# A two-layer kernel with routed adapters: item places a block sooner, column numbers in portions, B remainders last in VectorE's step, last-layer weights rounded in pieces

## Chip, cores and metric

One NeuronCore of a Trainium2 chip. The metric is the device time of one execution in microseconds; lower is better.

## What is computed

64 items of 32 tokens with 512 features pass through two residual layers, all in f32. Cut to what matters:

```python
# layer 0: per item one of 8 matrices, then a linear layer with per-group LoRA
c  = einsum('bsi,boi->bso', x, weight[itok_B_3_7])
x  = x + c @ kernel + bias + lora0(c) + lora_shared(c)
# layer 1: per item one of 16 adapters on gate, up and down of a SiLU layer (512 -> 1376 -> 512)
gate = x @ W_gate.T + 0.5 * lora(x, A_gate[id], B_gate[id])
up   = x @ W_up.T   + 0.5 * lora(x, A_up[id],   B_up[id])
act  = silu(gate) * up
h    = act @ W_down.T + 0.5 * lora(act, A_down[id], B_down[id])
# last: a linear layer (W, b) and a LoRA whose rank (8, 16, 32, 64) is picked by softmax scores
x  = x + h @ W.T + b + routed_lora(h)
```

## The kernel before

**Split products.** Every f32 operand is kept as two fp32r parts. ScalarE rounds (`high`: a copy into the `_hi` tile), then VectorE or GpSimd subtracts (`low`: `x - hi` into the `_lo` tile), and TensorE makes three matmuls of one product (`product`: hi*hi, hi*lo, lo*hi; lines 1332 to 1334) or two where one side is stacked (`stacked`, lines 1338 and 1339).

**Stages.** (1) The per-item matrices of layer 0, to about 86 us; results go through DRAM, sorted by item. (2) The first layer, `first_layer(t)` for four blocks t of 512 tokens: TensorE turns the tokens (`turn_h0`), forms the LoRA product in the bank `psX`, then four output chunks `kern(o)`, `lora(o)` in `psD`; VectorE's `add(o)` (line 1113) adds bias and `x_all` and writes x back to `x_all`. From about 98 to 169 us. (3) The expert layer, `body(t)` for four blocks, 22 steps each (chunks of 128 of the 1376 features; the middle of the steps is a hardware loop). Its items are sorted by adapter, so the columns of a block in `x_all` are 16 items at places known only at run time. To about 645 us. (4) The last layer, four blocks.

**Item places.** A chain of small VectorE operations works out how the items are sorted by adapter: `rank_items`, `place_fillers`, `place_items` (ends in `perm1`), two tiny matmuls on TensorE into `psX` (lines 1471, 1472), and `item_places` (writes `item1_at`, the column of each item, and `mask1`). Beside it `gather_rows` writes the row tables by which GpSimd gathers adapter rows from DRAM (`fixed`: `fix_a`, `fix_b`; `rows`: `ab`). These pieces are spread over VectorE's program of the first layer: `gather_rows` and `rank_items` in block 1 before `add(0)`, `place_fillers` in block 1 after `add(2)`, `place_items` in block 2, the tiny matmuls after `kern(0)` of block 3, `item_places` in block 3. `block_cols(eng, t)` (line 425) loads the 16 column numbers of a block into registers of an engine: four loads from memory and eight register instructions behind each (line 429). ScalarE does this for block 0 before `high_at(0)` (line 766), VectorE in block 3 after `add(1)`, ahead of `low_at(0)`, `low_bu(0, 0)` and `add(2)`, `add(3)`.

**From the first layer to the expert layer.** When all 16 `add`s are done (`x1_f`), ScalarE rounds the 16 items of expert block 0 (`high_x1`, `x_hi`), VectorE subtracts (`low_x1`, `x_lo`), and TensorE starts `ranks(0)`, 24 products with the gathered A rows (`at_hi`, `at_lo`) into `psX`.

**A step of the expert layer**, number n. ScalarE: rounds the next gate and up weights (`gu_hi`) and the next B rows (`bu_hi` of step n+1), then the A_down rows of this step (`ad_hi`, out of `psX`), `dn_hi`, then `silu`, then `act_hi`. VectorE: `low_bu` of step n+1 (tile `bu`), then the remainder of `ad`, then `act_f` = up * silu, then `act_lo`. GpSimd: `gu_lo`, `dn_lo`, then the gathers of `ab` two steps ahead. TensorE, step n: waits for the `ad` remainder of step n-1, turns the A_down rows of this step into `psX` (line 1545), 12 matmuls for gate, 12 for up, the LoRA parts that need `bu`, then the down product of step n-1. In step 0 of a block the turn stands between gate and up, and in step 0 of block 2 ScalarE and VectorE also split the last layer's weights: `wf` (128x2048), `ra` (128x272), `rb`, all at once.

**Start of the last layer.** The last products of the expert layer in `psD` are put back into item order in `h_all` by `put_h`: ScalarE copies chunks 0 and 1 (semaphore `h_out0`), VectorE chunks 2 and 3 (`h_out1`). Then `high_h(0)`, `low_h(0)` split them (`hta_hi`, `hta_lo`), and TensorE begins. Both engines wait for both semaphores first.

The order on every engine is written out by hand, semaphores alone tie the engines together.

## Time and profile before

| | |
|---|---|
| median of 3 runs | 723.53 us (723.34 to 724.62) |
| the profiled execution, its own time | 725.0 us |
| its span, first to last instruction | 723.1 us |
| TensorE / weight loads | 95% / 79% busy |
| VectorE / ScalarE / GpSimd | 48% / 40% / 44% busy |
| mean granted TensorE clock | 0.991 |
| chain that ended last | TensorE 84%, VectorE 4%, DMA 3%, issue 3%, ScalarE 2% |

In the profile, PE is TensorE, PEld its weight loads, DVE VectorE, ACT ScalarE, POOL GpSimd, SP the queue of plain DMAs. L12 is line 12 of the kernel; most subtractions have line 853 (VectorE) or 554 (GpSimd) and most roundings line 639, since helpers issue them, so the tile names tell them apart. Idle time of an engine that is not the bottleneck costs nothing. Times within the text are microseconds from the span's start.

### The profile page before, as it was taken

To read this page: it belongs to the slowest core of one execution; us is meant where nothing else is said; L and a number is where in the kernel's file an instruction comes from. 1 tells how busy PE (TensorE), PEld (TensorE's weight loads), DVE (VectorE), ACT (ScalarE), POOL (GpSimd) and SP (SyncE) were. 2 spreads that over 40 slices of the span, in tenths; PEclk is the share of its full clock that TensorE was granted. 3 is DMA by queue.
4 is the path that set the end of the run, shared out by engine and by line. 5 is a ranking of instruction groups with operands and counts; after the bars stand their busy time and mean duration, and the time that the engine had idled before them with its cause. 6 is when DMAs were issued, how large, how long until landed. Compare 5 with 4: busy or idle time off the path is not lost.

```text
span 723.1 us, 11495 instructions
## 1 busy us (share of the span) xinstructions
PE 689.0 (95%) x3432; PEld 574.2 (79%) x3432; DVE 350.6 (48%) x716; ACT 286.0 (40%) x605; POOL 317.4 (44%) x266
## 2 busy tenths in 40 slices
PE   4799999997999999999999989999999999979997
PEld 3588888886788888888888868888888888867775
DVE  3788676644622442642343672344263244334564
ACT  2775542213543333543333564333354333333210
POOL 0133400301777665486665387666548666300000
PEclk9999999998999999999999999999999999998999
DMA  8974451301244336244434225433424533100113
GB/s 297 362 263 159 164 203 59 103 0 45 80 154 142 112 103 227 90 128 146 123 109 139 88 90 155 127 112 107 146 88 133 152 113 112 51 2 0 59 63 112
DMA packets 30801, 88.90 MB, mean 123 GB/s; under 512 B 4609, under 2 KB 4737, under 8 KB 29217
## 3 DMA queue, kind: packets, MB, share of 16 engines
q1 hardware_dynamic: 21936, 61.05, 25.5%
q0 software_dynamic: 8672, 27.27, 12.0%
q8 instruction: 22, 0.36, 0.2%
q14 instruction: 27, 0.21, 0.1%
q10 hardware_dynamic: 144, 0.00, 0.0%
HBM read 78.35 MB, written 9.96 MB: 122 GB/s over the span
## 4 chain that ended last, share of the span: by engine, by line
PE 84%; DVE 4%; DMA 3%; issue 3%; ACT 2%; DVEq 1%; POOL 1%; ACTq 0%; SPq 0%; POOLq 0%
PE psD L1332 10%; PE psD L1333 10%; PE psD L1334 9%; PE psG L1332 6%; PE psG L1334 5%; PE psG L1333 5%; PE psU L1333 5%; PE psU L1334 5%; PE psU L1332 5%; PE psX L1332 2%; PE psX L1333 2%; PE psX L1334 2%; PE psD L1402 2%; PE psD L1403 1%; PE psD L1404 1%
## 5 line engine op out<-in xcount | busy, mean ns | idle before, releaser
L554 POOL TENSOR_TENSOR gu_lo<-gu_raw,gu_hi 128x1024 fp32r<-128x1024 f32 x44 | 107.8, 2451 | 130.9 <-ACT gu_hi L639 130.7
L853 DVE TENSOR_TENSOR bu<-ab,bu 64x512 fp32r<-64x512 f32 x44 | 74.8, 1699 | 74.5 <-ACT bu L639 74.3
L589 POOL DMA_INDIRECT ab<-in_ab,idx_row x88 | 87.0, 989 | 47.8 <-POOL idx_row L583 34.3
L1228 DVE TENSOR_TENSOR act_f<-psU,silu 128x512 f32<-128x512 f32 x44 | 30.4, 691 | 139.8 <-ACT silu L796 139.8
L796 ACT ACTIVATE silu<-psG 128x512 f32<-128x512 f32 x44 | 26.2, 596 | 148.3 <-PE psG L1339 143.2
L554 POOL TENSOR_TENSOR dn_lo<-dn_raw,dn_hi 128x512 fp32r<-128x512 f32 x44 | 67.4, 1533 | 30.6 <-ACT dn_hi L639 29.9
L1332 PE MATMUL psG<-x_hi,gu_hi 128*128 128x512 f32 x176 | 72.8, 414 | 0.2
L1332 PE MATMUL psD<-act_hi,dn_hi 128*128 128x512 f32 x176 | 69.0, 392 | 0.0
L1333 PE MATMUL psD<-act_lo,dn_hi 128*128 128x512 f32 x176 | 69.0, 392 | 0.0
L1333 PE MATMUL psG<-x_lo,gu_hi 128*128 128x512 f32 x176 | 68.9, 392 | 0.0
L1334 PE MATMUL psG<-x_hi,gu_lo 128*128 128x512 f32 x176 | 68.9, 392 | 0.0
L1332 PE MATMUL psU<-x_hi,gu_hi 128*128 128x512 f32 x176 | 68.8, 391 | 0.0
L1334 PE MATMUL psD<-act_hi,dn_lo 128*128 128x512 f32 x176 | 68.6, 390 | 0.0
L1334 PE MATMUL psU<-x_hi,gu_lo 128*128 128x512 f32 x176 | 68.5, 389 | 0.0
L1333 PE MATMUL psU<-x_lo,gu_hi 128*128 128x512 f32 x176 | 68.5, 389 | 0.0
L559 POOL DMA_INDIRECT h_scratch<-h,idx_s x22 | 23.8, 1082 | 63.7 <-ACT h L668 32.4
L639 ACT ACTIVATE gu_hi<-gu_raw 128x1024 fp32r<-128x1024 f32 x44 | 46.1, 1048 | 4.0 <-DMA gu_raw<-in_gu 4.0
L639 ACT ACTIVATE act_hi<-act_f 128x512 fp32r<-128x512 f32 x44 | 27.8, 632 | 45.8 <-DVE act_f L1228 45.8
L853 DVE TENSOR_TENSOR act_lo<-act_f,act_hi 128x512 fp32r<-128x512 f32 x44 | 30.6, 696 | 30.7 <-ACT act_hi L639 30.7
L639 ACT ACTIVATE bu<-ab 128x512 fp32r<-128x512 f32 x44 | 27.4, 622 | 36.7 <-DMA ab<-in_ab,idx_row 36.7
L1402 PE MATMUL psD<-cond_w_hi,xs_t_hi 128*128 x88 | 35.5, 404 | 5.6 <-DVE cond_w_lo L853 5.6
L1334 PEld LDWEIGHTS psG<-x_hi,gu_lo 128*128 128x128 f32 x176 | 33.2, 189 | 7.7
(323 smaller groups left out, 1594.1 us busy)
## 6 DMA issues: line engine op xcount, KB each, us to landing
gu_raw<-in_gu SPq DMA_DIRECT2D x44, 512.0 KB, 3.5
dn_raw<-in_dn SPq DMA_DIRECT2D x44, 256.0 KB
cond_w_raw<-in_cond_w SPq DMA_DIRECT2D x8, 1024.0 KB, 8.1
x_all<-in_x_t SPq DMA_DIRECT2D x4, 1024.0 KB, 11.2
tok<-h_scratch SPq DMA_DIRECT2D x4, 1024.0 KB, 5.6
out_t<-x_all SPq DMA_DIRECT2D x16, 256.0 KB, 2.2
ab<-in_ab,idx_row POOLq DMA_INDIRECT x88, 3.2
kraw<-in_kern SPq DMA_DIRECT2D x1, 1024.0 KB, 14.2
```

The costliest lines, as they stand in the source:

```text
L554: pool.tensor_tensor(dst, x, hi, ALU.subtract).then_inc(s, 1)
L559: pool.indirect_dma_start(h0_dram, bass.IndirectOffsetOnAxis(idx_s[:, b:b + 1], 0), h0[:, ring, :], None).then_inc(S[f"c_st{ring}"], 16)
L589: pool.indirect_dma_start(ab[:, par, g, :], None, a["ab"], bass.IndirectOffsetOnAxis(idx_row[:, par, g:g + 1], 0)).then_inc(S[f"ab_in{par} ...
L639: act.activation(dst, x, ACT.Copy).then_inc(s, 1)
L796: act.activation(silu[:], psG[:], ACT.Silu).then_inc(S["silu_s"], 1)
L853: dve.tensor_tensor(dst, x, hi, ALU.subtract).then_inc(s, 1)
L1228: dve.tensor_tensor(act_f[:], psU[:], silu[:], ALU.mult).then_inc(S["act_f_s"], 1)
L1332: pe.matmul(ps, wh, xh, start=start, stop=False, skip_group_check=True)
L1333: pe.matmul(ps, wh, xl, start=False, stop=False, skip_group_check=True)
L1334: return pe.matmul(ps, wl, xh, start=False, stop=stop, skip_group_check=True)
L1402: pe.matmul(ps, xh, w[0], start=c == 0, stop=False)
L1403: pe.matmul(ps, xl, w[0], start=False, stop=False)
```

## The change

1. VectorE: `place_fillers` moves ahead of `add(0)` in block 1, `place_items` and `gather_rows` to behind `add(2)` of block 1, `item_places` to block 2. TensorE: the two tiny matmuls move from block 3 to block 2, and `turn_h0(3)`, which overwrites `psX`, now waits for `item1_ready` and `mask1_ready`.
2. The column numbers of block 0 on VectorE: eight are loaded behind `add(2)` of block 2, eight ahead of `add(0)` of block 3, none between `add(1)` and `low_at(0)`. On ScalarE all 16 are loaded in block 3 behind the rounding of `r64`.
3. `low_bu` is VectorE's last operation of a step in place of its first.
4. The last layer's weights are split in four pieces: half of `wf` in step 0 of block 2, half in step 0 of block 3, `ra` in the step before the last of block 2, `rb` in that of block 3.
5. ScalarE rounds chunks 0 and 1 of `high_h(0)` as soon as its own copies are done, chunks 2 and 3 after VectorE's.

```diff
--- before.py
+++ after.py
@@ -422,10 +422,11 @@
                                                              min_val=0, max_val=TOKENS - ITEM_T)
             return at
 
-        def block_cols(eng, t):
+        def block_cols(eng, t, part=range(TB // BT)):
 
             cols = []
-            for b in range(TB // BT * t, TB // BT * (t + 1)):
+            for q in part:
+                b = TB // BT * t + q
                 _, at = nc.values_load_multi_w_load_instructions(item1_at[0:1, b * BI:b * BI + BI], engines=[eng.engine],
                                                                  min_val=0, max_val=TOKENS - ITEM_T)
                 cols += at
@@ -734,6 +735,9 @@
             for t in range(NTB):
                 act.wait_ge(S["t0_m"], t + 1)
                 high(r64_hi[:], r64_a[:], S["t0_hi"])
+                if t == 3:
+                    act.wait_ge(S["item1_ready"], 1)
+                    taken = block_cols(act, 0)
                 if t < NTB - 1:
                     act.wait_ge(S["t0_ps"], t + 1)
                     high(doubled(ae_hi), ae_of(t + 1), S["ae_s"])
@@ -762,8 +766,6 @@
                     act.activation(h_all[:, 0:2, bass.ds(col, ITEM_T)], psD[:, 0:2, i:i + ITEM_T], ACT.Copy
                                    ).then_inc(S["h_out0"], 1)
 
-            act.wait_ge(S["item1_ready"], 1)
-            taken = block_cols(act, 0)
             high_at(0)
             high_gu(0, 0, 0)
             high_bu(0, 1)
@@ -787,6 +789,10 @@
                     high(ad[:, par, :], psX[:, 0:NGT * P], S["ad_hi_s"])
                     act.wait_ge(S["dn_in"], 16 * (n + 1))
                     high(dn_hi[:, par, :], dn_raw[:], S["dn_hi_s"])
+                    if last(fc, 1) and t == 2:
+                        high(ra_hi[:], ra_raw[:], S["wf_hi_s"])
+                    if last(fc, 1) and t == 3:
+                        high(rb[:], rb_raw[:], S["wf_hi_s"])
                     if last(fc, 1) and t < NTB - 1:
                         taken.extend(block_cols(act, t + 1))
                     if last(fc):
@@ -800,11 +806,10 @@
                         act.wait_ge(S["fix_in"], 64 * (t + 1))
                         act.wait_ge(S["h_ps"], C * t)
                         high(bd_hi[:], fix_b[:], S["bd_hi_s"])
-                    if first and t == 2:
+                    if first and t > 1:
                         act.wait_ge(S["late_in"], 64)
-                        high(wf_hi[:], wf_raw[:], S["wf_hi_s"])
-                        high(ra_hi[:], ra_raw[:], S["wf_hi_s"])
-                        high(rb[:], rb_raw[:], S["wf_hi_s"])
+                        half = slice(2 * t - 4, 2 * t - 2)
+                        high(wf_hi[:, half], wf_raw[:, half], S["wf_hi_s"])
 
                 chunks(act, step, 1, 1)
 
@@ -828,10 +833,10 @@
             def high_h(t):
                 act.wait_ge(S["lin_ps"], max(t - 1, 0))
                 for c in range(C):
+                    if t == 0:
+                        act.wait_ge(S[f"h_out{c // 2}"], ITEMS)
                     high(HT2[t % 2][0][:, c, :], h_all[:, c, tokens_of(t)], S["h_hi_s"])
 
-            act.wait_ge(S["h_out0"], ITEMS)
-            act.wait_ge(S["h_out1"], ITEMS)
             high_h(0)
             high_h(1)
             for t in range(NTB):
@@ -1126,26 +1131,28 @@
                 if t == 0:
                     fill_bins()
                 if t == 1:
-                    gather_rows()
                     rank_items()
+                    dve.wait_ge(S["small_in"], 32)
+                    place_fillers()
                 if t == 2:
-                    place_items()
+                    item_places()
                 if t == 3:
-                    item_places()
+                    taken.extend(block_cols(dve, 0, (2, 3)))
                 add(0)
                 add(1)
                 if t < NTB - 1:
                     low_h0(t + 1)
                 else:
-                    taken.extend(block_cols(dve, 0))
                     low_at(0)
                     low_bu(0, 0)
                 add(2)
                 if t == 0:
                     find_fillers()
                 if t == 1:
-                    dve.wait_ge(S["small_in"], 32)
-                    place_fillers()
+                    place_items()
+                    gather_rows()
+                if t == 2:
+                    taken.extend(block_cols(dve, 0, (0, 1)))
                 add(3)
 
             def low_at(t):
@@ -1212,8 +1219,6 @@
                 def step(fc, j, par):
                     n = NF * t + fc
                     first = isinstance(fc, int) and fc == 0
-                    if not last(fc):
-                        low_bu(1 - par, n + 1)
                     dve.wait_ge(S["ad_hi_s"], n + 1)
                     lower_ad = ad[:, par, :].rearrange("p (g k n) -> p g k n", g=NGT, k=2)[:, :, 1, :]
                     low(lower_ad, psX[:, 0:NGT * P].rearrange("p (g k n) -> p g k n", g=NGT, k=2)[:, :, 1, :], lower_ad,
@@ -1228,10 +1233,17 @@
                     dve.tensor_tensor(act_f[:], psU[:], silu[:], ALU.mult).then_inc(S["act_f_s"], 1)
                     dve.wait_ge(S["act_hi_s"], n + 1)
                     low(act_lo[:, par, :], act_f[:], act_hi[:, par, :], S["act_lo_s"])
-                    if first and t == 2:
-                        dve.wait_ge(S["wf_hi_s"], 3)
-                        low(wf_lo[:], wf_raw[:], wf_hi[:], S["wf_lo_s"])
+                    if not last(fc):
+                        low_bu(1 - par, n + 1)
+                    if first and t > 1:
+                        dve.wait_ge(S["wf_hi_s"], 2 * t - 3)
+                        half = slice(2 * t - 4, 2 * t - 2)
+                        low(wf_lo[:, half], wf_raw[:, half], wf_hi[:, half], S["wf_lo_s"])
+                    if last(fc, 1) and t == 2:
+                        dve.wait_ge(S["wf_hi_s"], 2)
                         low(ra_lo[:], ra_raw[:], ra_hi[:], S["wf_lo_s"])
+                    if last(fc, 1) and t == 3:
+                        dve.wait_ge(S["wf_hi_s"], 4)
                         low(rb[RMAX:2 * RMAX], rb_raw[RMAX:2 * RMAX], rb[RMAX:2 * RMAX], S["wf_lo_s"])
 
                 chunks(dve, step, 1, 1)
@@ -1434,6 +1446,9 @@
 
                 pe.wait_ge(S[f"h0_in{t % 2}"], 16 * (t // 2 + 1))
                 pe.wait_ge(S["t0_m"], t)
+                if t == 3:
+                    pe.wait_ge(S["item1_ready"], 1)
+                    pe.wait_ge(S["mask1_ready"], 1)
                 for c in range(C):
                     for s in range(SUB):
                         mm = pe.transpose(H0_BANK[c][:, s * P:s * P + P], TOK[t % 2][:, s, c * P:c * P + P], ident)
@@ -1465,8 +1480,8 @@
                     mm = product(psX[:], both(ae_hi, ae_lo, al, c, al), both(hi, lo, al, c, al), c == 0, c == C - 1)
                 mm.then_inc(S["t0_ps"], 1)
                 kern(0)
-                if t == NTB - 1:
-                    pe.wait_ge(S["t0_m"], NTB)
+                if t == 2:
+                    pe.wait_ge(S["t0_m"], t + 1)
                     pe.wait_ge(S["perm1_s"], 1)
                     pe.matmul(psX[:, 0:ITEMS], cst("item_no", ITEMS), perm1[:], start=True, stop=True)
                     pe.matmul(psX[:, ITEMS:2 * ITEMS], cst("ones", ITEMS), perm1_f[:], start=True, stop=True
@@ -1501,8 +1516,7 @@
 
             def ranks(t):
 
-                pe.wait_ge(S["item1_ready"], 1)
-                pe.wait_ge(S["mask1_ready"], 1)
+                pe.wait_ge(S["t0_m"], NTB)
                 pe.wait_ge(S["ad_lo_s"], NF * t)
                 pe.wait_ge(S["at_lo_s"], NGT * (t + 1))
                 for g in range(NGT):
@@ -1639,7 +1653,7 @@
                     stacked(psD[:, o, :], rb[:, o * P:o * P + P], r64_hi[:], r64_lo[:], False, True
                             ).then_inc(S["out_ps"], 1)
 
-            pe.wait_ge(S["wf_lo_s"], 3)
+            pe.wait_ge(S["wf_lo_s"], 4)
             routed(0)
             for t in range(NTB):
                 second_layer(t)
```

The order of VectorE's instructions in block 3 of the first layer, before, from `item_places` on (r_a, be, r_lo stand just ahead of it; the pair of rows `TENSOR_LOAD`, `ISA x8` is one portion of four columns and stands four times):

```order
L1007 TENSOR_SCALAR item_at<-psX 1x64
L1009 TENSOR_TENSOR slot_102<-psX,const 128x64
L1010 TENSOR_SCALAR mask_121<-slot_102,const 128x64
L1113 SCALAR_TENSOR_TENSOR x_all<-psD,bias,x_all 128x512 x2
L429 TENSOR_LOAD item_at
L429 ISA x8
L853 TENSOR_TENSOR at_lo<-psG,at_hi 128x512
L853 TENSOR_TENSOR at_lo<-psU,at_hi 128x512
L853 TENSOR_TENSOR bu<-ab,bu 64x512
L1113 SCALAR_TENSOR_TENSOR x_all<-psD,bias,x_all 128x512 x2
```

And now, from `add(3)` of block 2 on; here the portion stands twice, and twice more just ahead of the first row:

```order
L1118 SCALAR_TENSOR_TENSOR x_all<-psD,bias,x_all 128x512
L1123 TENSOR_TENSOR r_a<-psX,const 128x512
L858 TENSOR_TENSOR be<-b_eff,be 64x512
L858 TENSOR_TENSOR r_lo<-r_a,r_hi 128x512
L430 TENSOR_LOAD item_at
L430 ISA x8
L1118 SCALAR_TENSOR_TENSOR x_all<-psD,bias,x_all 128x512 x2
L858 TENSOR_TENSOR at_lo<-psG,at_hi 128x512
L858 TENSOR_TENSOR at_lo<-psU,at_hi 128x512
L858 TENSOR_TENSOR bu<-ab,bu 64x512
L1118 SCALAR_TENSOR_TENSOR x_all<-psD,bias,x_all 128x512 x2
```

The loads have left the place between the first and the second pair of `add`s.

VectorE, steps 0 and 1 of block 2 of the expert layer, before:

```order
L853 TENSOR_TENSOR bu<-ab,bu 64x512
L853 TENSOR_TENSOR ad<-psX,ad 128x2x64
L1228 TENSOR_TENSOR act_f<-psU,silu 128x512
L853 TENSOR_TENSOR act_lo<-act_f,act_hi 128x512
L853 TENSOR_TENSOR wf_lo<-wf_raw,wf_hi 128x2048
L853 TENSOR_TENSOR ra_lo<-ra_raw,ra_hi 128x272
L853 TENSOR_TENSOR rb<-rb_raw,rb 64x512
L413 UNCONDITIONAL_BRANCH
L413 ISA
L853 TENSOR_TENSOR bu<-ab,bu 64x512
L1217 REGISTER_ALU
L853 TENSOR_TENSOR ad<-psX,ad 128x2x64
```

And now, the same stretch:

```order
L1233 TENSOR_TENSOR act_f<-psU,silu 128x512
L858 TENSOR_TENSOR act_lo<-act_f,act_hi 128x512
L858 TENSOR_TENSOR bu<-ab,bu 64x512
L858 TENSOR_TENSOR wf_lo<-wf_raw,wf_hi 128x1024
L413 UNCONDITIONAL_BRANCH
L413 ISA
L858 TENSOR_TENSOR ad<-psX,ad 128x2x64
```

Between `act_lo` of step 0 and `ad` of step 1 four long operations stood; now two stand there, `bu` and half of `wf_lo`.

## Rows read from the trace of the kernel before

**Rows 1.** The page, part 1: TensorE's busy time, share of the span, instructions.

```profile
PE 689.0 (95%) x3432; PEld 574.2 (79%) x3432; DVE 350.6 (48%) x716; ACT 286.0 (40%) x605; POOL 317.4 (44%) x266
```

**Rows 2.** Waits of TensorE: who for whom, us in total, times, longest.

```profile
PE psX L1332 <- DVE x_lo L853: 5.0, 1, 5.0
...
PE psX L1545 <- DVE ad L853: 4.4, 3, 2.7
...
PE psX L1332 <- DVE hta_lo L853: 4.0, 1, 4.0
```

**Rows 3.** Timeline, VectorE, first layer's end: start, us, operation, idle before.

```profile
161.55 1.41 DVE L1113 SCALAR_TENSOR_TENSOR x_all<-psD,bias,x_all 128x512 f32<-128x512 f32 x2 [2.77 <-PE psD L1339]
...
168.31 0.69 DVE L853 TENSOR_TENSOR at_lo<-psG,at_hi 128x512 fp32r<-128x512 f32 x1 [5.35 <-issue]
...
170.35 1.41 DVE L1113 SCALAR_TENSOR_TENSOR x_all<-psD,bias,x_all 128x512 f32<-128x512 f32 x2
```

**Rows 4.** Timeline, TensorE, the same stretch.

```profile
174.25 0.55 PE L1332 MATMUL psX<-x_hi,at_hi 128*128 128x256 f32 x1 [5.01 <-DVE x_lo L853]
```

**Rows 5.** Timeline, VectorE, blocks 2 and 3 of the first layer.

```profile
140.29 0.22 DVE L995 SCALAR_TENSOR_TENSOR there<-own_in,is_own,hit_at 64x16 f32<-64x16 f32 x1
...
152.13 0.75 DVE L1113 SCALAR_TENSOR_TENSOR x_all<-psD,bias,x_all 128x512 f32<-128x512 f32 x1 [2.42 <-PE psD L1339]
```

**Rows 6.** Timeline, GpSimd, its first subtraction after the gathers.

```profile
165.47 2.39 POOL L554 TENSOR_TENSOR gu_lo<-gu_raw,gu_hi 128x1024 fp32r<-128x1024 f32 x1 [29.16 <-ACT gu_hi L639]
```

**Rows 7.** Timeline, TensorE, ScalarE and VectorE, first steps of the expert layer.

```profile
187.78 0.41 PE L1545 MATMUL psX<-const,ab 128*128 128x128 f32 x2 [0.92 <-DVE ad L853]
...
198.69 0.44 PE L1545 MATMUL psX<-const,ab 128*128 128x128 f32 x2 [0.84 <-DVE ad L853]
...
186.90 0.60 ACT L796 ACTIVATE silu<-psG 128x512 f32<-128x512 f32 x1
...
194.50 3.81 DVE L853 TENSOR_TENSOR bu<-ab,bu 64x512 fp32r<-64x512 f32 x1 [4.88 <-ACT bu L639]
```

**Rows 8.** Timeline around 424 to 434 us: ScalarE, VectorE, GpSimd, TensorE.

```profile
423.51 1.90 ACT L639 ACTIVATE wf_hi<-wf_raw 128x2048 fp32r<-128x2048 f32 x1
...
428.73 2.63 DVE L853 TENSOR_TENSOR ra_lo<-ra_raw,ra_hi 128x272 fp32r<-128x272 f32 x1
...
424.23 2.42 POOL L554 TENSOR_TENSOR bd_lo<-fix_b,bd_hi 128x1024 fp32r<-128x1024 f32 x1
...
434.01 0.44 PE L1545 MATMUL psX<-const,ab 128*128 128x128 f32 x2 [2.69 <-DVE ad L853]
```

**Rows 9.** Windows: us, busy time of each engine, PEclk, DMA share, GB/s.

```profile
169.00:174.00 5.00, 0.24 (x2) 0.00 (x0) 4.30 (x13) 2.12 (x11) 0.00 (x0) 0.95 0.44 154
...
180.00:183.00 3.00, 3.00 (x15) 2.25 (x14) 2.87 (x5) 0.93 (x2) 0.00 (x0) 0.94 0.00 0
...
431.00:434.00 3.00, 0.31 (x2) 0.00 (x0) 2.94 (x5) 0.00 (x0) 2.22 (x4) 1.00 0.54 159
...
645.00:649.00 4.00, 0.42 (x4) 0.21 (x2) 2.59 (x17) 2.22 (x13) 0.00 (x0) 0.87 0.01 2
...
652.00:655.00 3.00, 3.00 (x9) 1.82 (x8) 0.00 (x0) 0.28 (x2) 0.00 (x0) 0.53 0.00 0
```

**Rows 10.** Timeline, start of the last layer: VectorE, ScalarE, TensorE.

```profile
645.57 2.20 DVE L1201 COPY h_all<-psD 128x64 f32 x16 [3.65 <-PE psD L1334]
...
647.85 2.19 ACT L639 ACTIVATE hta_hi<-h_all 128x512 fp32r<-128x512 f32 x4 [1.78 <-issue]
...
649.45 0.66 PE L1332 MATMUL psX<-hta_hi,ra_hi 128*68 128x512 f32 x1 [4.04 <-DVE hta_lo L853]
```

**Rows 11.** VectorE: `bu` at line 853 (ns, min/median/max), and one steady step.

```profile
L853 DVE TENSOR_TENSOR bu<-ab,bu x44: 683/2100/3807, 169.6 to 619.4; 64x512 fp32r<-64x512 f32 x44
...
343.14 0.69 DVE L853 TENSOR_TENSOR act_lo<-act_f,act_hi 128x512 fp32r<-128x512 f32 x1 [0.70 <-ACT act_hi L639]
...
351.72 0.69 DVE L1228 TENSOR_TENSOR act_f<-psU,silu 128x512 f32<-128x512 f32 x1 [4.30 <-ACT silu L796]
```

## The prediction

> **What bounds the kernel now.** I read the page first: TensorE is busy 95% of the span [rows 1], so the time is its matmuls plus what it stands idle; the edits add and remove no matmul. Then the waits of TensorE alone. Besides the start of the program, which the change leaves alone, there are three entries of size [rows 2]: once 5.0 us for VectorE's `x_lo`, three times together 4.4 us for the `ad` remainder, once 4.0 us for `hta_lo`. All three name VectorE, which is busy under half the time: it is late, not slow. So the timeline of VectorE before each wait, for what held it there. At the end of the first layer it is idle for 5.35 us before `at_lo` with "issue" as the releaser [rows 3]: its sequencer loads 16 column numbers. In step 1 of the expert layer a `bu` takes 3.81 us ahead of `ad` [rows 7]; at 428.73 `ra_lo`, 272 columns, takes 2.63 us [rows 8]. Last, the windows, for the granted clock around the pauses [rows 9].
>
> **The sum, part by part**, against the profiled execution's own 725.0 us (span 723.1 and 1.9 around it). That execution is 1.5 us above the median of the runs, which spread over 1.3 us.
>
> *Columns in portions.* `add(2)` and `add(3)` of the last block stand behind the loads and end at 170.35 + 1.41 = 171.76 [rows 3]. TensorE's last product ended at 174.25 - 5.01 = 169.24 [rows 4], and one `add` takes 0.75 [rows 5], so `add(3)` can end at 170.0. What moves up in front of it (`at_lo` twice and `bu`, 0.7 each, or up to 3.8 for the `bu` if GpSimd holds it up as in [rows 7]) fits between 163 and 169.2. Everything behind it (`x_hi`, `x_lo`, TensorE) follows. Gain **1.7**; bounds 0 and 1.8. The loads are still made: eight cost half of 5.35, 2.7 us. Eight go into 2.42 us of idle time ahead of `add(3)` of block 2 [rows 5], 0.3 late and with nobody waiting, since `kern(3)` of the next block is the first to need it; eight ahead of `add(0)` of block 3, where VectorE is idle for 2.77 [rows 3] and `item_places` has gone. Cost 0; if a cover were gone, what overruns is paid, 0.3.
>
> *Places a block sooner.* Small operations of some 0.2 us [rows 5]. The fullest slot is the one behind `add(2)` of block 1: twelve, 2.4 us, in a slot that in block 2 is idle for 2.42 [rows 5]. The gathers of GpSimd start some 10 us later, since `gather_rows` now stands behind them; GpSimd is idle for 29.16 before it next has work [rows 6], which covers it. The two tiny matmuls cost the same in block 2 as in block 3. The new wait of `turn_h0(3)` is for three operations of 0.2 us that VectorE does while TensorE is at `kern(1)`. All 0; bound for the wait 0.6.
>
> *`bu` last.* It takes 0.69 alone; the median is 2.1, the worst 3.81 [rows 11], since VectorE is held while GpSimd subtracts. Today that time lies ahead of `ad`, for which the turn of the next step waits. Twice at the start this shows: 0.92 at 187.78 and 0.84 at 198.69 [rows 7]. The first can't all be won: the gate matmuls behind the turn overwrite `psG`, which `silu` reads until 186.90 + 0.60 = 187.50, and without the wait the turn would stand at 186.86. I take **0.4** (0 to 0.9). The second is free: **0.9** (0.8 to 1.0, with the refill of the array). Elsewhere `ad` is done long before the turn, so nothing. What is late next is `bu` itself: it is needed 6 us into the next step, and there it runs some 8 us earlier than that.
>
> The Trainium skill, "SBUF — State Buffer", section "SBUF: two separate sides", says that VectorE with two SBUF inputs and GpSimd take one port pair as a lock, and whoever starts first keeps it for the whole instruction. By that rule a moved `bu` and a moved half of `wf` only pick another instruction to wait for, and a long one; the 3.81 above agrees, with two GpSimd operations in a row. That is the third rival.
>
> *Weights in pieces.* `ad` of step 1 in block 2 stands behind `wf_lo`, `ra_lo`, `rb`, `bu`; TensorE waits 2.69 and restarts at 434.01 [rows 8], so it wanted it at 431.32. Now half of `wf` stands there. ScalarE's rounding ends at 423.51 + 0.95 = 424.5; VectorE then finds GpSimd in `bd_lo` until 424.23 + 2.42 = 426.65; half of `wf` is 1024 columns, twice a 0.69, so 1.4, to 428.0: 3 us to spare. Gain **2.8** (1.0 to 2.9, the low end below). Block 3 gets the other half in the same place with the same spare: 0. `ra` and `rb` come in late steps, where VectorE is idle for 4.30 per step [rows 11]: 0; at most 0.4 for the `ra` rounding ahead of ScalarE's column loads.
>
> *Start of the last layer.* ScalarE's own copies end at 647.85 - 1.78 = 646.07; it then waits for VectorE's, done at 645.57 + 2.20 = 647.77, rounds, and VectorE subtracts [rows 10]. Now the first rounding is done by then, and the subtraction (0.7) runs from 647.8 to 648.5. TensorE starts at 648.6, not 649.45: **0.85** (0.6 to 0.9).
>
> *The clock.* In the 5.01 us pause the granted clock fell to half (1.2 GHz): 0.95 over 169 to 174 puts the fall at 173.5, 0.94 over 180 to 183 the return at 180.4 [rows 9]. So TensorE worked 6.1 us at half rate, 3.05 lost, of which some 2.1 count (the gate work at its end would wait for `silu` anyway). In the 4.04 us pause 0.87 over 645 to 649 puts the fall at 648.0, only 2.5 us into it, and 0.53 over 652 to 655 the return at 654.8: 5.4 us at half rate, 2.7 lost. In the 2.69 us pause it stayed at 1.00. The two pauses shrink to 3.3 and 3.2, between the one that kept its clock and the two that lost it. I give each even odds and count one of the two: **2.4** (0 to 4.8).
>
> The sum: 1.7 + 0.4 + 0.9 + 2.8 + 0.85 = 6.65 of idle time, 718.35; with the clock kept once, 715.95. Forecast **716.0**.
>
> **Rivals.**
> *Both pauses still lose the clock:* 718.3. For it: a fall came after only 2.5 us of idle. Against: 2.69 did not bring one.
> *Both keep it:* 725.0 - 6.65 - 4.8 = 713.5. The Trainium skill, "TensorE: Matmul & The Clock Gate", section "HAM oscillation — how this bites in real kernels", ties the fall to an idle gap beyond a limit; read strictly this case would be the likeliest. The trace doesn't bear it out fully: the fall at 648.0 came early in its pause.
> *The halves wait for the port:* in steps 0 and 1 of blocks 2 and 3 GpSimd has `bd_lo`, `gu_lo` and `dn_lo` behind one another. If VectorE loses twice more, by 2.4 and 1.5, half of `wf` ends at 431.9 and `ad` at 432.2, 0.9 late; twice, so 1.8 of the 2.8 is given back: 717.8. For it the 3.81 [rows 7], against it the median of 2.1 [rows 11], one loss.
> *The first layer's end isn't set by the loads:* if `add(3)` comes no sooner, 1.7 is missing: 717.7. Against: "issue" is a releaser nothing else explains.
> *Slower:* `bu` last is held by GpSimd in every step and pushes `act_f` of the next. From `act_lo`'s end, 343.83, to the next `act_f`, 351.72, are 7.9 us [rows 11]; `bu` and `ad` alone need 1.0. It decides from a hold of 6.9 us on, or when `bu`'s end delays GpSimd's gathers, which wait for it; past that point each 0.1 us in some 84 steps is 8 us, so 724.3 and more. The worst hold is 3.81 less 0.69, 3.1.
>
> **Numbers.** Forecast (all steps, clock kept once) 0.45; both lose it 0.22; both keep it 0.15; the halves wait 0.12; the first layer's end 0.03; slower 0.03. The range has to take in both clock cases, the port, and the median's 1.5 below the profiled run: 712.8 (the 713.5, a little lower for that) to 719.4 (the 718.3 with half of the port's 1.8 on it). About 0.2%, 1.4 us, is what a measurement here can tell from no change. All cases but one gain over 4 us: faster 0.95, same 0.02, slower 0.03.
>
> **What would show it.** TensorE's wait for `x_lo` at 3.3 or less and no 5 us "issue" on VectorE; no `ad` wait over 0.6 in the whole trace; the wait for `hta_lo` at 3.2; the clock back at 1.00 in one of the two windows behind these pauses; `bu` with a median near 0.7 to 1.0. I am wrong if TensorE waits at the turn of step 2 in block 2 or 3 (port), if `turn_h0(3)` waits for `mask1`, or if the gain is over 5 us at other places than these five.

## The result, and the profile after

| | before | after |
|---|---|---|
| median | 724.08 us (723.34 to 726.23, 4 runs) | **715.8 us** (714.46 to 718.78, 4 runs) |
| the profiled execution, its own time | 725.0 us | 718.78 us |
| its span | 723.1 us | 716.9 us |
| mean granted TensorE clock there | 0.991 | 0.990 |

The ratio is 0.9882, 95% interval 0.9863 to 0.9902: 8.3 us gained, forecast 716.0. The four runs of after spread over 4.3 us, those of before over 2.9. The same kernel was run six times more in another set (a0 below): 719.05 (714.78 to 719.6). All ten together have a median of 717.2, so the gain is nearer 7 us than 8.3 if they count alike. The spread comes back below: most of it is the clock, but not all.

The page and TensorE's waits first, kernel after, as in [rows 1, 2]; columns of the waits: us in total, times, longest.

```profile
PE 690.0 (96%) x3432; PEld 574.7 (80%) x3432; DVE 316.4 (44%) x717; ACT 286.2 (40%) x606; POOL 314.1 (44%) x266
```

```profile
PE psX L1344 <- DVE hta_lo L858: 3.3, 1, 3.3
PE psX L1344 <- DVE x_lo L858: 3.3, 1, 3.3
...
PE psG L1344 <- ACT silu L802: 0.6, 1, 0.6
PE psX L1559 <- DVE ad L858: 0.5, 2, 0.3
```

TensorE does the same 3432 matmuls. Its three large waits were 5.0, 4.4 and 4.0 us; now they are 3.3, 0.5 and 3.3. What is left of the first and the third is the chain of rounding, subtraction and restart itself. VectorE is busy 34 us less, with one more instruction: `bu` went from 74.8 to 32.1 us in all, and the two halves of `wf_lo` take 13.5 where the whole took 2.5. This is the view of one tile (ns, min/median/max), where [rows 11] had 683/2100/3807:

```profile
L858 DVE TENSOR_TENSOR bu<-ab,bu x44: 689/690/2476, 164.5 to 622.9; 64x512 fp32r<-64x512 f32 x44
```

The instruction is the same. Formerly it started while GpSimd was in `gu_lo` and sat through it; most of its busy time was waiting. A steady step of the kernel before, VectorE, then GpSimd:

```profile
354.57 2.48 DVE L853 TENSOR_TENSOR bu<-ab,bu 64x512 fp32r<-64x512 f32 x1 [0.77 <-ACT bu L639]
```

```profile
354.10 2.40 POOL L554 TENSOR_TENSOR gu_lo<-gu_raw,gu_hi 128x1024 fp32r<-128x1024 f32 x1 [2.71 <-ACT gu_hi L639]
356.46 1.74 POOL L554 TENSOR_TENSOR dn_lo<-dn_raw,dn_hi 128x512 fp32r<-128x512 f32 x1
```

Here `bu` gets in between the two subtractions of GpSimd, and `dn_lo` takes 1.74 in place of 1.28. In the steady steps this waiting cost TensorE nothing; it did so at the two step starts of block 0 and, together with the last layer's weights, in block 2.

*End of the first layer.* Timeline of VectorE, kernel after (start, us, operation, idle before), against [rows 3]:

```profile
161.06 1.41 DVE L1118 SCALAR_TENSOR_TENSOR x_all<-psD,bias,x_all 128x512 f32<-128x512 f32 x2 [3.76 <-PE psD L1351]
162.59 0.69 DVE L858 TENSOR_TENSOR at_lo<-psG,at_hi 128x512 fp32r<-128x512 f32 x1
163.19 0.68 DVE L858 TENSOR_TENSOR at_lo<-psU,at_hi 128x512 fp32r<-128x512 f32 x1
164.54 2.48 DVE L858 TENSOR_TENSOR bu<-ab,bu 64x512 fp32r<-64x512 f32 x1 [0.66 <-ACT bu L640]
167.05 0.75 DVE L1118 SCALAR_TENSOR_TENSOR x_all<-psD,bias,x_all 128x512 f32<-128x512 f32 x1
168.78 0.75 DVE L1118 SCALAR_TENSOR_TENSOR x_all<-psD,bias,x_all 128x512 f32<-128x512 f32 x1 [0.99 <-PE psD L1351]
170.17 2.92 DVE L858 TENSOR_TENSOR x_lo<-x_all,x_hi 128x128 fp32r<-128x128 f32 x14 [0.63 <-ACT x_hi L640]
```

And TensorE, against [rows 4]:

```profile
172.02 0.55 PE L1344 MATMUL psX<-x_hi,at_hi 128*128 128x256 f32 x1 [3.27 <-DVE x_lo L858]
```

The "issue" of 5.35 us is gone. The last `add` waits for TensorE's last product (0.99), so nothing of VectorE's own is late: pause 5.01 to 3.27, 1.74 gained. Even the `bu` that a GpSimd operation held for 2.48 was covered.

*Blocks 2 and 3.* VectorE, then GpSimd, then TensorE at the turns of step 2 in block 2 and in block 3, against [rows 8]:

```profile
419.69 0.69 DVE L858 TENSOR_TENSOR bu<-ab,bu 64x512 fp32r<-64x512 f32 x1
420.87 6.74 DVE L858 TENSOR_TENSOR wf_lo<-wf_raw,wf_hi 128x1024 fp32r<-128x1024 f32 x1 [0.48 <-ACT wf_hi L640]
427.52 0.28 DVE L858 TENSOR_TENSOR ad<-psX,ad 128x128 fp32r<-128x128 f32 x1
```

```profile
420.52 2.40 POOL L555 TENSOR_TENSOR bd_lo<-fix_b,bd_hi 128x1024 fp32r<-128x1024 f32 x1
422.88 2.39 POOL L555 TENSOR_TENSOR gu_lo<-gu_raw,gu_hi 128x1024 fp32r<-128x1024 f32 x1
425.24 1.28 POOL L555 TENSOR_TENSOR dn_lo<-dn_raw,dn_hi 128x512 fp32r<-128x512 f32 x1
```

```profile
427.86 0.44 PE L1559 MATMUL psX<-const,ab 128*128 128x128 f32 x2 [0.27 <-DVE ad L858]
...
544.50 0.44 PE L1559 MATMUL psX<-const,ab 128*128 128x128 f32 x2 [0.26 <-DVE ad L858]
```

Half of `wf_lo` is 1024 columns, which VectorE does in 1.23 us when it is alone (the run with late weights shows it, below). Here it starts 0.35 us behind `bd_lo` and takes 6.74: GpSimd does three subtractions back to back, and VectorE gets in only when the last has ended, at 426.5. In the kernel before there was a gap of 0.63 us between `bd_lo` and `gu_lo`, since ScalarE rounded all the last layer's weights ahead of `gu_hi`; the whole `wf_lo`, waiting on `bd_lo`, got in there and took 2.52. With half of that rounding `gu_hi` is ready before `bd_lo` ends, and the gap is gone. The wait of 2.69 became 0.27, and block 3 has a new one of 0.26.

*Start of the last layer*, ScalarE and TensorE, against [rows 10]:

```profile
640.55 1.15 ACT L640 ACTIVATE hta_hi<-h_all 128x512 fp32r<-128x512 f32 x2
642.18 1.15 ACT L640 ACTIVATE hta_hi<-h_all 128x512 fp32r<-128x512 f32 x2 [0.49 <-DVE h_all L1208]
```

```profile
643.07 0.67 PE L1344 MATMUL psX<-hta_hi,ra_hi 128*68 128x512 f32 x1 [3.28 <-DVE hta_lo L858]
```

Two of the four roundings now come ahead of VectorE's copies. Pause 4.04 to 3.28, 0.76 gained.

*The clock.* Windows, kernel after (us, busy time of each engine, granted clock, DMA share, GB/s), against [rows 9]:

```profile
167.00:172.00 5.00, 1.75 (x8) 1.14 (x7) 3.35 (x13) 2.34 (x12) 0.00 (x0) 0.89 0.47 159
172.00:175.00 3.00, 2.98 (x14) 3.00 (x15) 1.49 (x8) 0.96 (x5) 0.00 (x0) 0.50 0.00 0
175.00:178.00 3.00, 3.00 (x15) 2.85 (x15) 0.41 (x1) 0.00 (x0) 0.00 (x0) 0.54 0.00 0
178.00:181.00 3.00, 2.96 (x14) 2.14 (x13) 2.88 (x5) 1.16 (x2) 0.00 (x0) 1.00 0.00 0
...
643.00:646.00 3.00, 2.93 (x7) 1.68 (x8) 1.74 (x3) 2.41 (x5) 0.00 (x0) 0.50 0.03 8
646.00:649.00 3.00, 3.00 (x9) 1.87 (x8) 0.00 (x0) 0.53 (x1) 0.00 (x0) 0.53 0.00 0
649.00:652.00 3.00, 3.00 (x17) 2.27 (x16) 0.20 (x2) 2.02 (x3) 0.00 (x0) 1.00 0.00 0
```

In this execution the clock fell to half (1.2 GHz) in both pauses, as before, and stayed there for 6.8 us each time. So this profile, 718.78, is the first rival's case ("both pauses still lose the clock", 718.3), and the median of the runs, 715.8, is not.

### The profile page after: what moved, and what is told of

The parts are those of the page before. It is cut to its first block and busy times, and to the rows that moved or that the text cites. A ratio compares the mean times of both kernels' runs of the same rounds, so it can differ in the third digit from the quotient of the medians.

```text
span 716.9 us, 11498 instructions
## 1 busy us (share of the span) xinstructions
PE 690.0 (96%) x3432; PEld 574.7 (80%) x3432; DVE 316.4 (44%) x717; ACT 286.2 (40%) x606; POOL 314.1 (44%) x266
## 5 line engine op out<-in xcount | busy, mean ns | idle before, releaser
L555 POOL TENSOR_TENSOR gu_lo<-gu_raw,gu_hi 128x1024 fp32r<-128x1024 f32 x44 | 112.5, 2557 | 117.4 <-ACT gu_hi L640 116.5
L555 POOL TENSOR_TENSOR dn_lo<-dn_raw,dn_hi 128x512 fp32r<-128x512 f32 x44 | 56.7, 1288 | 31.4 <-ACT dn_hi L640 31.4
L858 DVE TENSOR_TENSOR ad<-psX,ad 128x128 fp32r<-128x128 f32 x44 | 12.8, 291 | 74.1 <-ACT ad L640 73.9
```

Of the source, the lines that this page charges most:

```text
L555: pool.tensor_tensor(dst, x, hi, ALU.subtract).then_inc(s, 1)
L858: dve.tensor_tensor(dst, x, hi, ALU.subtract).then_inc(s, 1)
```

## The experiments

Each is an edit of the kernel after. Three sets of runs, each with the kernel before beside it on the same chip: a0, e1, e2, e3 (before 724.18, 723.13 to 726.15); e4, e5, e6, e7 (before 725.35); e8, e9 (before 724.58).

| | edit | us, median (range) | ratio to before, 95% interval |
|---|---|---|---|
| a0 | none: the kernel after | 719.05 (714.78 to 719.6) | 0.9908 (0.9883 to 0.9932) |
| e1 | `bu` first in the step | 720.47 (717.96 to 722.55) | 0.9948 (0.9931 to 0.9966) |
| e2 | 16 column numbers at once | 719.41 (717.96 to 720.3) | 0.9925 (0.991 to 0.994) |
| e3 | last layer's weights at once | 718.66 (716.24 to 720.47) | 0.9925 (0.9909 to 0.994) |
| e4 | `high_h(0)` waits for both | 717.15 (716.12 to 721.19) | 0.9896 (0.9872 to 0.9919) |
| e5 | unread matmuls in both pauses | 713.6 (713.28 to 714.25) | 0.9842 (0.9826 to 0.9858) |
| e6 | halves of `wf` late in the block | 716.36 (713.1 to 717.63) | 0.9867 (0.9845 to 0.9889) |
| e7 | e5 and e6 | **712.72** (712.02 to 713.69) | 0.983 (0.9813 to 0.9847) |
| e8 | before, unread matmuls in its pauses | 720.32 (718.32 to 721.75) | 0.9938 (0.9919 to 0.9957) |
| e9 | e7 with 5 unread matmuls, not 12 | 713.22 (712.49 to 715.84) | 0.9844 (0.9826 to 0.9861) |

**a0, the kernel after again.**

> The changed kernel again, to see how far its time and its clock move from run to run. If the two pauses of 3.27 us decide by luck whether the clock falls: runs between 713.5 and 718.8, and those with a mean clock of 0.990 are the long ones. If the clock always falls in both, all runs lie within 1 us of 718.

The mean clock that each run granted sorts the ten runs of this kernel. Four are at 0.990 and take 718.8 to 719.6; one at 0.993, 718.6; one at 0.995, 715.9; four at 0.997, 714.5 to 715.8. So the clock doesn't always fall in both; the runs reach 0.8 us further up than expected. The windows of the profiled one say what stands behind such a number:

```profile
167.00:172.00 5.00, 2.37 (x11) 1.64 (x9) 3.35 (x9) 1.72 (x9) 0.09 (x1) 1.00 0.47 159
172.00:175.00 3.00, 2.35 (x16) 2.32 (x17) 2.12 (x11) 1.58 (x8) 0.00 (x0) 0.87 0.00 0
175.00:178.00 3.00, 3.00 (x14) 2.83 (x14) 0.76 (x2) 0.00 (x0) 0.00 (x0) 0.56 0.00 0
178.00:181.00 3.00, 3.00 (x15) 2.22 (x14) 2.91 (x5) 1.54 (x3) 0.00 (x0) 1.00 0.00 0
```

Here the clock held through the whole pause, fell at 174.2, 1.5 us after TensorE had restarted at 172.65, and was back after 3.4 us, half of the 6.8 in the kernel after's first profile. The pause is the same 3.3 us.

The clock isn't the whole spread. TensorE's last product of the first layer ended at 171.0 in e6's profile, at 168.2 in e4's and at 168.1 in e5's, with the clock at 1.00 up to there and the same program. Between e6 and e5 1.6 us of this stands there early: TensorE's wait for `cond_w_lo` ends at 23.2 and at 21.6. The rest is open. So e6's profiled run took 716.9 with a mean clock of 0.998, and the kernel before spreads over 3 us (723.1 to 726.2) at 0.990 to 0.991.

**e1, `bu` back to the front of the step.**

```diff
                 def step(fc, j, par):
+                    if not last(fc):
+                        low_bu(1 - par, n + 1)
                     dve.wait_ge(S["ad_hi_s"], n + 1)
...
-                    if not last(fc):
-                        low_bu(1 - par, n + 1)
```

> The changed kernel with the B remainder ahead of ad again. My theory: the waits for ad return at steps 0 and 1 of block 0 (0.3 and 1.1 us), and since the bu of step 1 of blocks 2 and 3 comes after the half of wf, these waits grow by about 0.7 each: 2 to 3 us slower than the changed kernel, and bu has a median of 2 us again. Rival, bu's place does not matter (only the weights in pieces did): within 0.5 us of the changed kernel, no wait for ad over 0.5.

TensorE's waits, and VectorE in steps 0 and 1 of block 0:

```profile
PE psX L1559 <- DVE ad L858: 4.0, 4, 1.1
```

```profile
181.28 2.48 DVE L858 TENSOR_TENSOR bu<-ab,bu 64x512 fp32r<-64x512 f32 x1 [0.78 <-ACT bu L640]
183.78 0.29 DVE L858 TENSOR_TENSOR ad<-psX,ad 128x128 fp32r<-128x128 f32 x1
...
190.99 3.77 DVE L858 TENSOR_TENSOR bu<-ab,bu 64x512 fp32r<-64x512 f32 x1 [4.93 <-ACT bu L640]
194.79 0.29 DVE L858 TENSOR_TENSOR ad<-psX,ad 128x128 fp32r<-128x128 f32 x1
```

The two waits of [rows 7] are back (0.91 and 0.85), and those behind `wf_lo` grew from 0.27 and 0.26 to 1.10 each, since `bu` now stands behind the half as well. Its waits are 4.0 us where the kernel after has 0.5 for `ad` and 0.6 for `silu`: moving `bu` is worth 2.9 us, more than the 1.3 put down for it, because part of its worth lies in blocks 2 and 3. The median is only 1.4 us above a0, since its runs granted more clock (0.991 to 0.997). At equal clock, 0.997, the runs are 3.1 us apart (718.0 and 718.8 against 714.8 and 715.8), and in the two traces, each with one short fall here, the stretch from the restart of `ranks(0)` to that of the last layer is 3.2 us longer (473.3 against 470.1).

**e2, the column numbers in one piece.**

```diff
-                if t == 3:
-                    taken.extend(block_cols(dve, 0, (2, 3)))
...
                 else:
+                    taken.extend(block_cols(dve, 0))
                     low_at(0)
...
-                if t == 2:
-                    taken.extend(block_cols(dve, 0, (0, 1)))
```

> The changed kernel with VectorE's 16 column loads between add(1) and low_at(0) again, all else kept (places sooner, ScalarE's loads sooner). My theory: the pause before x_lo is 5.0 us again, 1.7 us slower; the clock falls there for certain. Rival, it was the earlier item places or ScalarE's earlier loads that helped: pause 3.3 us, no difference.

VectorE, then TensorE:

```profile
168.97 0.69 DVE L858 TENSOR_TENSOR at_lo<-psG,at_hi 128x512 fp32r<-128x512 f32 x1 [5.35 <-issue]
```

```profile
174.91 0.55 PE L1341 MATMUL psX<-x_hi,at_hi 128*128 128x256 f32 x1 [5.01 <-DVE x_lo L858]
```

Both numbers of before, to the hundredth, though `item_places` had gone to block 2: the loads made the pause, and moving the places alone brings nothing here. By the clock (0.995 in five of its six runs: after the 5.0 us pause of the profiled one it fell for 3.4 us only) this kernel was luckier than a0, and so its median is only 0.4 us above. (The five runs at 0.995 still lie 2.3 us apart, which the clock doesn't explain.) The pause is read from the trace, not from the medians.

**e3, the last layer's weights at once.**

```diff
-                    if first and t > 1:
-                        dve.wait_ge(S["wf_hi_s"], 2 * t - 3)
-                        half = slice(2 * t - 4, 2 * t - 2)
-                        low(wf_lo[:, half], wf_raw[:, half], wf_hi[:, half], S["wf_lo_s"])
+                    if first and t == 2:
+                        dve.wait_ge(S["wf_hi_s"], 3)
+                        low(wf_lo[:], wf_raw[:], wf_hi[:], S["wf_lo_s"])
```

(`ra` and `rb` behind it, and ScalarE's roundings likewise.)

> The changed kernel with all of the last layer's weights split at step 0 of block 2 again, bu last kept. My theory: VectorE is held by GpSimd's three operations in a row and then has wf (2.4 us), ra and rb to do, so the wait for ad at step 2 of block 2 is 2.7 us or more (before 2.69, now 0.27), block 3 has none: 2 to 3.5 us slower. Rival, bu last alone took the wait away: wait under 1 us.

```profile
427.18 0.44 PE L1551 MATMUL psX<-const,ab 128*128 128x128 f32 x2 [2.10 <-DVE ad L855]
```

2.10 comes back, not 2.69, because `bu` no longer stands between `rb` and `ad` (0.68 in the kernel before) but ahead of `wf_lo`, and block 3 has no wait. So of the pieces' 2.4 us in the trace 0.6 belongs to `bu`. The median doesn't show the loss that was expected, 2 to 3.5 us: it is 0.4 under a0's. At equal clock the runs are some 1 to 2 us slower (716.2 against 714.5 to 715.8 at 0.997, 720.0 and 720.5 against 718.8 to 719.6 at 0.990). A `wf_lo` of 2048 columns took 2.52 us here, less than the 6.74 of its half in the kernel after: it started at 420.1, when `bd_lo` had 0.4 us to go, and got into the gap of 0.63 ahead of `gu_lo`. Now GpSimd's `gu_lo` is the one that sits, 3.78 us in place of 2.39:

```profile
421.05 3.78 POOL L555 TENSOR_TENSOR gu_lo<-gu_raw,gu_hi 128x1024 fp32r<-128x1024 f32 x1 [0.63 <-ACT gu_hi L640]
```

Starting to wait first is not enough: in the kernel after `wf_lo` waited from 420.87, two microseconds before `gu_lo` started, and got in last. Here GpSimd left a gap.

**e4, the two waits of `high_h(0)` together.**

```diff
+            act.wait_ge(S["h_out0"], ITEMS)
+            act.wait_ge(S["h_out1"], ITEMS)
             high_h(0)
```

> The changed kernel with ScalarE waiting for both halves of h_all before the first rounding of the last layer. My theory: that pause is 4.0 us again and not 3.3, 0.8 us slower when the clock is the same in both. Rival, the subtraction on VectorE is held by its own copies anyway: pause 3.3, no difference.

```profile
642.48 0.42 PE L1344 MATMUL psX<-hta_hi,ra_hi 128*68 128x512 f32 x1 [4.04 <-DVE hta_lo L858]
```

The 4.04 of [rows 10] is back. The median, 717.15, can't be set against others at this size, for the clock's share differs.

**e5, no idle TensorE in the two pauses.** Twelve matmuls into a free bank, read by nobody, ahead of the wait for `x_lo` and as many ahead of that for `hta_lo`.

```diff
             def ranks(t):
+                if t == 0:
+                    for k in range(12):
+                        pe.matmul(psT[:], be[:, 0:P], r64_hi[:], start=True, stop=True, skip_group_check=True)
```

> The changed kernel with 12 matmuls of 128x512 whose results nobody reads in each of the two pauses (ahead of ranks(0) and ahead of the last layer), into psT. My theory: TensorE's idle time there falls from 3.27 to about 0.5 us, the clock never falls, and the 2.2 and 2.6 us that a long stretch at half rate costs are gone: all runs within 1 us of one another, near 714.0. Rival, the spread of the runs is not the clock's but the loads' at the start: the runs still spread by 3 us or more, median near 717.

```profile
167.00:172.00 5.00, 4.44 (x22) 3.50 (x21) 3.38 (x15) 3.02 (x16) 0.00 (x0) 1.00 0.44 151
172.00:175.00 3.00, 3.00 (x24) 2.84 (x23) 1.14 (x6) 0.29 (x2) 0.00 (x0) 1.00 0.00 0
...
639.00:643.00 4.00, 3.46 (x16) 2.00 (x15) 2.88 (x7) 3.24 (x6) 0.00 (x0) 1.00 0.00 2
643.00:646.00 3.00, 3.00 (x15) 2.17 (x13) 0.00 (x0) 2.55 (x3) 0.00 (x0) 1.00 0.00 0
```

The clock stays at 2.4 GHz and the five runs lie within 1.0 us, where the ten of the kernel after spread over 5.1. Their starts happened to agree as well (e7 spreads over 1.7, e8 over 3.4), so the other reading in the expectation, that the start moves the runs, is true for a part. The data comes no sooner after TensorE's last product; only the rate behind it changes. This is the forecast's rival "both keep it", 713.5, in every run.

**e6, the halves of `wf` in the last-but-one steps of blocks 1 and 2,** `ra` and `rb` in that of block 3, where GpSimd has one subtraction at a time.

```diff
-                    if first and t > 1:
+                    if last(fc, 1) and t in (1, 2):
...
-                        half = slice(2 * t - 4, 2 * t - 2)
+                        half = slice(2 * t - 2, 2 * t)
```

> The changed kernel with the halves of wf in the step before the last of blocks 1 and 2, ra and rb in that of block 3, where GpSimd issues gathers or nothing. My theory: the half of wf, which takes 6.74 us behind three GpSimd operations now, takes 1.3, the two waits of 0.27 for ad are gone with their refill, 0.8 us less up to the last layer. Rival, that half meets the same lock in the late step and moves the wait to the end of the block: no gain or a new wait at ranks.

```profile
L857 DVE TENSOR_TENSOR wf_lo<-wf_raw,wf_hi x2: 1224/1226/1227, 391.4 to 507.6; 128x1024 fp32r<-128x1024 f32 x2
```

1.23 us for the instruction that took 6.73, in both blocks, and no wait for `ad` is left. The 5.5 us between them was waiting on GpSimd's three subtractions. The time over the whole, 716.36, is blurred by clock and start; e7 against e5 shows the gain.

**e7, both.**

> Both of the last two at once, leaving nothing out of the result: if they add, 713.2, all runs within 1 us, faster than the changed kernel's 715.8 to 719.05. If the half-clock stretches come back by another pause, the spread of 3 us returns.

712.72 with 1.7 us of spread, 0.9 under e5, which is what the two waits of 0.27 with their refills cost (these two kernels' runs spread over 1.0 and 1.7 us, so this is rough). The traces agree: from the restart of `ranks(0)` to that of the last layer e5 takes 468.96 and e7 467.80, 1.2 less. It beats before and after.

**e8, the kernel before with its pauses filled** (20 and 16 unread matmuls), so that it can be set against e5 without the clock.

> The kernel before, with unread matmuls put into its two long pauses (20 ahead of x_lo, 16 ahead of h_all); nothing else is changed. It takes the clock out of the comparison: with the kernel after that had its pauses filled (713.6 us) it differs only by idle time. If my sum of idle times is right (pauses 1.74 and 0.76, about 1.4 at the two step starts, the halves' waits 2.4 of block 2 less about 0.5 of block 3), the change is worth about 5.5 to 6.2 us without any clock, so this one runs 719.1 to 719.8, with all its runs within about 1.2 us. Rival: a good part of the change's gain is clock it loses less often; then this one runs under 717.6 and the difference is under 4 us. Should it run above 721, the unread matmuls themselves cost something here.

```profile
PE psX L1548 <- DVE ad L853: 4.4, 3, 2.7
...
PE psX L1332 <- DVE x_lo L853: 0.5, 1, 0.5
...
PE psX L1332 <- DVE hta_lo L853: 0.4, 1, 0.4
```

The median is 720.32, so the two pauses cost before 4.3 us of clock, and between this and e5's 713.6 lie 6.7 us. That is more than the 5.5 to 6.2 expected, and not idle time alone: it compares two sets of runs, and in the two profiled ones TensorE's last product of the first layer ended 1.2 us later here (169.2 against 168.1). Behind that point the traces, neither with a fall of the clock, differ by 5.8 us: 1.74 in the pause before `x_lo`, 4.02 from there to the restart of the last layer (472.98 against 468.96), nothing after. The spread of 3.4 us is wider than I expected. Three of the six runs granted 0.997, about what one short fall leaves; where it comes is open, since the profiled run isn't one of them (the pause of 2.69, which isn't filled, is a candidate and was not tried).

**e9, fewer unread matmuls.** Five in each pause, so that TensorE still stands idle for 2.1 us.

> The kernel with the B half's last layer rounded late (e6) and only 5 unread matmuls in each of the two long pauses instead of 12, so that some 2 us of each stay idle. If a shorter idle stretch is enough to keep the clock, it runs 712.7 like e7, with all its runs within 1.5 us. If 2 us of idle still make the clock fall in some executions, its runs spread over more than 2 us, and its median lies at 714 or above.

```profile
171.00:174.00 3.00, 1.77 (x13) 1.80 (x14) 2.70 (x14) 2.17 (x11) 0.00 (x0) 0.91 0.00 0
174.00:177.00 3.00, 3.00 (x15) 2.94 (x15) 0.16 (x1) 0.00 (x0) 0.00 (x0) 0.52 0.00 0
...
640.00:643.00 3.00, 1.75 (x5) 1.00 (x6) 2.81 (x7) 2.65 (x6) 0.00 (x0) 0.68 0.01 3
```

Neither case came out clean. The profiled run, 715.84, lost the clock for 3.4 us at both pauses. Of the other four three, at 0.999, took 712.5 to 713.2; the fourth, 714.71 at 0.998, may have lost it once (e6's profiled run reads 0.998 with one short fall). A pause of 2.1 us can keep the clock or lose it; one of 0.5 kept it in every run of e5.

## Why the prediction held, step by step

- **Columns in portions**, 1.7: 1.74 in the trace, and e2 brings exactly the old pause back. The loads that moved cost nothing, as said; the rival about the first layer's end is out.
- **Places a block sooner**, 0: `turn_h0(3)` never waits.
- **`bu` last**, 0.4 and 0.9: together 1.3. From the restart of `ranks(0)` to the turn of step 2 e8 takes 22.20 us and e5 20.88, both at full clock. After the first, TensorE waits 0.55 for `silu`, the limit named beforehand. In steady steps nothing, though `bu` is 43 us shorter in all. What the step missed is that `bu` also shortens the queue behind `wf_lo` (e1, e3). The slower rival's mechanism needed a hold of 6.9 us; the longest `bu` took 2.48, a hold of 1.8.
- **Weights in pieces**, 2.8: the wait went from 2.69 to 0.27 and block 3 got 0.26 plus the array's refill. The 3 us "to spare" didn't exist. The sum let VectorE wait for one GpSimd operation, as in the kernel before; it waited for three, because ScalarE's shorter rounding had closed the gap between them. This is the rival "the halves wait for the port", its mechanism came true in both blocks, and so did the sign of being wrong that was named for it, a wait at the turn of step 2. Its price was too high: 0.9 each time, the trace 0.3 and a refill, 0.9 to 1.2 for both by e5 against e7. Net the pieces brought about 1.9 of the 2.8 (the 4.02 of e8 against e5, less 1.3 for `bu` and 0.76 for the start of the last layer). The forecast's step was wrong in its reason and 0.9 too high in its size. The Trainium skill, "SBUF — State Buffer", section "SBUF: two separate sides", has VectorE with two SBUF inputs and GpSimd hold their shared port for a whole instruction. The traces agree: the same subtraction took 1.23 alone and 6.74 beside three. Whether the waiting engine gets in between two operations that follow back to back went both ways. `wf_lo` was never let in before the third had ended, in either block of after, a0, e1, e2, e4 and e5. In the kernel before `bu` got in behind `gu_lo` in the steady steps (2.48) and didn't in step 1 of blocks 0 and 1 (3.81 and 3.53). What decides is open.
- **Start of the last layer**, 0.85: 0.76, and e4 brings the old pause back.
- **Idle time in all**, 6.65: 5.8 in the traces of e8 and e5 (1.74 and 4.02). By medians e8 less e5 is 6.7; that this meets the forecast is in part a difference of their starts. The 0.9 that is missing is the step of the weights.
- **The clock**, 4.8 lost before and half of it kept: 4.3 lost before (before less e8) and 2.2 lost after (715.8 less e5's 713.6), so 2.1 kept, against 2.4. (This is by the first four runs; by the six of a0 nothing was kept.) But "kept or lost" was the wrong picture. Twelve unfilled pauses of 3.3 us stand in the profiles of after, a0, e1, e2, e3, e4 and e6. In three the clock was at half rate for 6.8 us, in six for 3.4, in three not at all. On average that is half of the full loss, so even odds gave the right mean for a wrong reason, and the median of four runs lay near it by luck: six more gave 719.05. The four runs at 0.990 take 718.8 to 719.6; the profiled one of them lost both pauses in full, and by their clock so did the others (forecast for that rival: 718.3). That is four runs in ten where I gave 0.22.

The Trainium skill, "TensorE: Matmul & The Clock Gate", section "HAM oscillation — how this bites in real kernels", ties the fall to an idle gap beyond a limit. The runs agree that shorter gaps lose less, taken over all: of the two of 5.0 us and the two of 4.0 each once 6.8 us and once 3.4 at half rate, the 3.3 us on average 3.4, that of 0.5 nothing. They don't agree that the length of the gap decides: the same 3.3 us gave all three outcomes, and a gap of 5.0 us gave the long fall in before and the short one in e2.

## What to carry to other kernels

When an engine that is busy under half its time is named as the releaser of every large wait, look at what stands in its queue ahead of that operation, register loads ("issue") included, and move it; nothing has to get faster. Of VectorE operations that GpSimd can hold up, place them by what GpSimd has queued there, and count all of it, not the one operation that is running: the same subtraction took 1.23 or 6.74 us. Count it as it will be after the change: less work on ScalarE let GpSimd's next operation follow without a gap. When runs of one kernel spread more than those of another, sort them by granted clock first, and compare two traces from one restart of TensorE to the next, which leaves the start out. Then fill the pauses that can't be removed with unread matmuls: the spread went from 5.1 to 1.0 us (1.7 in e7, 3.4 in e8) and the median from 717.2, that of all ten runs, to 713.6.

## What the runs showed of the hardware that was not expected

- After a pause of 3.3 us the clock may fall during it, or after TensorE has restarted (1.5 us after, in a0), or not at all; half rate then lasts 6.8 or 3.4 us, and no other length was seen. The same two lengths came after the pauses of 5.0 and 4.0. All five long stretches began 0.7 us or more before TensorE restarted; the ten short ones (two of them in e9's pauses of 2.1) began between 0.7 us before the restart and 1.5 after it. Why is open.
- A VectorE subtraction that starts behind a GpSimd one can wait for every GpSimd operation that follows without a gap: 6.74 us through `bd_lo`, `gu_lo` and `dn_lo` (2.40, 2.39, 1.28). It can also get in after the first: 2.48 for `bu` behind `gu_lo`, ahead of `dn_lo`.
- VectorE's busy time can be mostly waiting: `bu` went from a median of 2100 to 690 ns by its place alone.
